# Token ids spread from 16 partitions, the folded table copied by ScalarE, and transposes that wait chunk by chunk

## The reference

```
h = relu(conv(emb_table[x]))                  # x: (2, 1024) ids under 125; 128 features; 2 taps, groups of 4
h = h + attention(layernorm(h))               # 8 heads of 64; its residual is the normed input
h = h + ffn(layernorm(h))                     # attention-like product, 8 experts, last product
```

## Time and profile before

| | us |
|---|---|
| median of 3 runs (386.87 to 386.99) | 386.97 |
| the profiled execution | 386.93 |
| its span | 385.1 |
| TensorE busy (share of the span) | 378.7 (98%) |
| VectorE | 274.7 (71%) |
| ScalarE | 276.6 (72%) |
| GpSimd | 294.0 (76%) |

### The profile page before, as it was taken

The page is one execution under the profiler, slowest core; times in us unless marked ns, Lnnn a source line. Parts: engine busy times, 40 slices in busy tenths (PEclk is TensorE's granted clock), DMA queues, the critical chain, the costliest instruction groups (busy, mean ns, idle before and its releaser), DMA issues.

```text
span 385.1 us, 6735 instructions
## 1 busy us (share of the span) xinstructions
PE 378.7 (98%) x2368; PEld 221.7 (58%) x2368; DVE 274.7 (71%) x485; ACT 276.6 (72%) x396; POOL 294.0 (76%) x145
## 2 busy tenths in 40 slices
PE   8999999999999999999999999999999999999996
PEld 7866544544555445445544644454455744599995
DVE  6997777787877787777777787877785446775223
ACT  3566656668868886987788688868886489337763
POOL 3080486949999999999999999999999699900021
PEclk9999999999999999999999999999999999999999
DMA  4001002101132041103010720172044105000001
GB/s 133 22 0 49 8 5 53 55 0 57 33 82 56 3 98 16 55 3 110 3 55 5 217 56 3 33 188 58 4 109 113 57 1 147 19 2 15 14 29 55
DMA packets 28245, 19.46 MB, mean 51 GB/s; under 512 B 21264, under 2 KB 23696, under 8 KB 28212
## 3 DMA queue, kind: packets, MB, share of 16 engines
q1 hardware_dynamic: 27636, 18.05, 18.4%
q10 hardware_dynamic: 576, 0.98, 0.8%
HBM read 17.72 MB, written 1.17 MB: 49 GB/s over the span
## 4 chain that ended last, share of the span: by engine, by line
PE 95%; DVE 3%; ACT 1%; issue 1%; DVEq 0%
PE psum L694 30%; PE psum L683 24%; PE psum L621 11%; PE psum L609 6%; PE psum L630 4%; PE psum L738 4%; PE psum L749 3%; PE psum L585 3%; PE psum L705 2%; PE psum L560 1%; PE psum L646 1%; PE psum L648 1%; PE psum L772 1%; PE psum L534 1%; DVE attn_out L1096 1%
## 5 line engine op out<-in xcount | busy, mean ns | idle before, releaser
L1132 DVE TENSOR_REDUCE half_maxes<-psum 128x1 f32<-128x512 f32 x232 | 149.0, 684 | 26.1 <-PE psum L621 24.5
L895 ACT ACTIVATE probs<-psum 128x1024 f32<-128x1024 f32 x128 | 124.8, 1022 | 54.9 <-PE psum L683 54.4
L694 PE MATMUL psum<-probs,v_all 128*64 128x512 f32 x512 | 123.7, 604 | 0.0
L1362 POOL TENSOR_TENSOR sums<-sums,probs 128x1024 f32<-128x1024 f32 x31 | 74.2, 2393 | 3.8 <-ACT probs L895 3.8
L1362 POOL TENSOR_TENSOR odd_sum<-odd_sum,probs 128x1024 f32<-128x1024 f32 x31 | 74.3, 2396 | 0.0
L694 PEld LDWEIGHTS psum<-probs,v_all 128*64 128x64 f32 x512 | 31.2, 136 | 62.3 <-issue 41.9
L1180 DVE TENSOR_SCALAR psum<-max_plane 128x512 f32<-128x512 f32 (+1 forms) x55 | 43.0, 791 | 30.9 <-ACT probs L895 30.9
L1362 POOL TENSOR_TENSOR sums<-probs 128x1024 f32<-128x1024 f32 x16 | 38.0, 2374 | 26.9 <-ACT probs L895 26.4
L621 PE MATMUL psum<-k_round,q_round 64*128 64x512 f32 x256 | 57.8, 450 | 0.6 <-DVE half_maxes L1132 0.5
L621 PEld LDWEIGHTS psum<-k_round,q_round 64*128 64x128 f32 x256 | 24.1, 183 | 53.8 <-DVE half_maxes L1132 42.9
L683 PE MATMUL psum<-q_round,k_round 64*128 64x512 f32 x256 | 52.4, 404 | 0.1
(11 more groups left out here) (131 smaller groups left out, 451.5 us busy)
## 6 DMA issues: line engine op xcount, KB each, us to landing
max_plane<-rows_scratch SPq DMA_DIRECT2D x16, 512.0 KB, 3.9
inv_sb<-inv_scratch SPq DMA_DIRECT2D x14, 256.0 KB, 5.3
max_rows_of<-maxes SPq DMA_DIRECT2D x128, 0.5 KB, 2.0
v_all<-in_fc SPq DMA_DIRECT2D x4, 512.0 KB, 7.5
fc_late<-in_fc SPq DMA_DIRECT2D x4, 512.0 KB, 7.4
out_h<-probs SPq DMA_DIRECT2D x7, 128.0 KB, 1.8
v_all<-in_w ACTq DMA_DIRECT2D x3, 256.0 KB, 3.7
woT<-in_wo SPq DMA_DIRECT2D x1, 256.0 KB, 3.5
```

The lines of the kernel that those rows point to most:

```text
L694: last = pe.matmul(out_bank[head_rows(h), :], v_all[:, s, kc, head_rows(h)], probs[unit(s, kc, half) % TILES][:, h, :], start=(kc == 0), s ...
L895: last = act.activation(probs[u % TILES][:, heads, :], source, ACT.Exp, scale=SCALE)
L1132: dve.reduce_max(half_maxes[:, h, qc, keys:keys + 1], slot[:, h, :], AX.X).then_inc(maxed, 1)
L1362: pool.tensor_tensor(chain[:, :, :], first[:, :, :], probs[kc][:, :, :], ALU.add).then_inc(own, 1)
```

## The change

- The ids are loaded as 16 rows of 128, one row to a partition, and converted as 16x128. The selector has 16 columns.
- Each group is spread by four products of 128 columns, each with its own selector column, in place of one of 512. The semaphore is raised by the last of the four.
- The warm-up has four products in place of six.
- The folding product stands behind the first group's spreading products, ahead of the second group's. Its result is copied by ScalarE, ahead of the rounding of the K weights, and no longer by VectorE between the one-hot comparisons.
- Each of the first eight transposes waits for its own chunk, in place of one wait for four.
- ScalarE's fourth rectifier stands behind the two roundings of the first sequence.

```diff
-WARM_START = 6
+WARM_START = 4
-        ids_rows = residual[0:NG, 0:GROUP, :].rearrange("p t c -> p (t c)")
-        ids_whole, row_select = xL[:, 0:BANK], xL[:, BANK:BANK + NG]
+        ids_rows = residual[0:NCH, 0, :]
+        ids_whole, row_select = xL[:, 0:CHUNK], xL[:, CHUNK:CHUNK + NCH]
-            sp.dma_start(ids_rows.bitcast(I32), x.rearrange("b (g n) -> (b g) n", g=NG // B)).then_inc(ids_loaded, 16)
+            sp.dma_start(ids_rows.bitcast(I32), x.rearrange("b (g n) -> (b g) n", g=KCH)).then_inc(ids_loaded, 16)
             def spread_ids(g):
-                pe.matmul(bank(IDS_BANK[g]), row_select[:, g:g + 1].broadcast_to([128, 128]), ids_whole,
-                          start=True, stop=True).then_inc(ids_spread, 1)
+                for j in range(GROUP):
+                    row = g * GROUP + j
+                    last = pe.matmul(bank(IDS_BANK[g])[:, j * CHUNK:(j + 1) * CHUNK], row_select[:, row:row + 1].broadcast_to([128, 128]),
+                                     ids_whole, start=True, stop=True)
+                last.then_inc(ids_spread, 1)
             spread_ids(0)
-            spread_ids(1)
             pe.wait_ge(consts_made, 1)
             pe.wait_ge(tables_loaded, 16)
             pe.matmul(bank(3)[:, 0:TAPS * C], embT, convT, start=True, stop=True).then_inc(folded_ready, 1)
+            spread_ids(1)
             spread_ids(2)
             spread_ids(3)
             for g in range(NG // B):
-                pe.wait_ge(x_normed, GROUP * (g + 1))
-                x_to_features(g, bank(FEATURE_BANK[g])).then_inc(xt_filled, 1)
+                for j in range(GROUP):
+                    pe.wait_ge(x_normed, GROUP * g + j + 1)
+                    last = pe.transpose(bank(FEATURE_BANK[g])[:, j * CHUNK:(j + 1) * CHUNK], x1[:, g * GROUP + j, :], ident[:, :])
+                last.then_inc(xt_filled, 1)
+            act.wait_ge(folded_ready, 1)
+            act.copy(folded[:, :], bank(3)[:, 0:TAPS * C]).then_inc(folded_sb, 1)
             act.wait_ge(w_loaded, 48)
             relu(2)
-            relu(3)
             for g in range(NG // B):
                 act.wait_ge(xt_filled, g + 1)
                 x_round(g, bank(FEATURE_BANK[g]))
+            relu(3)
-            dve.tensor_copy(row_select, ident[:, 0:NG])
+            dve.tensor_copy(row_select, ident[:, 0:NCH])
-            dve.tensor_scalar(ids_whole[0:NG, :], ids_rows.bitcast(I32), float(VOCAB - 1), 0.0, ALU.min, ALU.add).then_inc(ids_made, 1)
+            dve.tensor_scalar(ids_whole[0:NCH, :], ids_rows.bitcast(I32), float(VOCAB - 1), 0.0, ALU.min, ALU.add).then_inc(ids_made, 1)
             make_onehot(0)
             make_onehot(1)
-            dve.wait_ge(folded_ready, 1)
-            dve.tensor_copy(folded[:, :], bank(3)[:, 0:TAPS * C]).then_inc(folded_sb, 1)
             make_onehot(2)
             make_onehot(3)
```

## The result

| | before | changed |
|---|---|---|
| median, us | 387.06 (386.87 to 387.53, 6 runs) | 389.54 (389.36 to 390.51, 6 runs) |
| the profiled execution, us | 386.93 | 390.51 |
| its span, us | 385.1 | 388.7 |

The ratio is 1.0067, 95% interval [1.0054, 1.008]: slower by 2.5 us in the medians (2.6 by the ratio), where 386.7 was forecast in a range up to 388.8. The profiled execution is the slowest of the six, so its rows show 3.6 us, and about one of them is the luck of that execution.

What follows compares the result with a forecast made beforehand. TensorE was taken to bound the kernel, with 95% of the span; +0.04 us up to the convolution and -0.24 from transposes and rectifier gave -0.20, so 386.7 us, with a range for 8 in 10 of 386.0 to 388.8.

Steps and rivals of the forecast that it cites:

- part 3: Sixteen spreading products for four: load-bound, 0.112 us each (0.215 at 1.2 GHz), rise kept at 5.05; sum +0.04 us.
- rival B: TensorE's clock: rise only after twelve spreading products and eight convolution records, 2.0 us lost, 388.7 us; 12%.
- Part 1: Ids on 16 partitions: conversion stands behind GpSimd's memset and ends at 3.24 us.
- Part 2: Warm-up of four: streams until 2.77 us, hole of about 0.5 us, first spreading weight load at 3.30.
- Part 4: Folded table copied by ScalarE: 0.38 us, over by 5.6 to 5.8, hidden before the convolution, costing nothing.
- Parts 5 and 6: Chunk-wise transposes of the second group and fourth rectifier behind the roundings: K products earlier, sum -0.24 us.
- Rivals A and C: Spreading products: A, priced like plain f32, 388.5 us, 20%; C, at the pace of their columns, 386.0 us, 12%.

Runs made afterwards that it cites:

- a: Changed kernel with six warm-up products instead of four: 387.47 us median, ratio 1.0019.
- j: Changed kernel with GpSimd's two large memsets waiting for the converted ids, ten runs: ratio 1.0037, five at 386.5 to 386.8 us or so, others from 388.7.
- k: Changed kernel with five warm-up products instead of four: 389.5 us in four of four runs.
- o: Changed kernel with five warm-up products, the same kernel as k run again: median 387.15 us, seven early and three late.
- l: Changed kernel run again with no edit: 389.56 us, ratio 1.007.
- m: Kernel of b with twelve rounded-type products of 128 columns added between the fold and the second spreading product: 389.6 us, ratio 1.0067.
- b: Changed kernel with ids on 4 rows of 512 and four 512-column spreading products again, warm-up still four: 386.86 us, ratio 0.999.
- c: Kernel before with four warm-up products instead of six, nothing else: 387.27 us, ratio 1.0004.
- e: Changed kernel with 4 rows of 512 ids, four 512-column spreading products and six warm-ups: 386.47 us, ratio 0.9983.
- f: Kernel before with only the chunk-wise transposes and the fourth rectifier behind the roundings: 386.73 us, ratio 0.9992.
- i: Kernel of e with GpSimd's two large memsets behind the converted ids and five warm-ups: 386.45 us, ratio 0.9983.
- d: Changed kernel with its sixteen small spreading products in plain f32: 388.74 us, ratio 1.0048.
- n: Kernel of b with six plain f32 products of 128 columns added between the fold and the second spreading product: 388.44 us, ratio 1.0038.
- h: Changed kernel with GpSimd's two large memsets waiting for the converted ids, a single execution: 386.8 us.

## Why the prediction was wrong

**The step that failed** is one sentence of part 3: "I leave that moment where it is", the rise at 5.05 us. In the profiled execution it came at 12.8. All else in the sum up to it held. I had seen that the small products stream for half of the time and had put it into rival B at 12%, and what I held against it spoke of a hole only. The runs give the products the greater weight. They are in every kernel that has late runs, at 388.7 us and above (changed, a, j, k/o, l, m), while b, c, e, f and i have 51 runs, none above 388.2. (d and n carry dearer or added plain products, so their times start higher; in their traces the rise is at 5.1 and 7.0.) The hole alone (c) costs 0.2 us in the medians, and under 0.6 by its interval. How often the small products delay the rise goes with what TensorE did before them: late were 10 of 10 runs after four warm-ups and a hole of 0.5 us, 6 of 11 with the hole at 0.2, 7 of 14 after five warm-ups without a hole, 3 of 10 after six, 0 of 10 after eight. This order isn't shown to be more than a tendency. The sets of runs are from several chips: on the one that ran a and o, both have three late of ten, with six and with five warm-ups, while on the one that ran k, l and j all of k and l are late and six of ten of j. The number of warm-ups and the hole are told apart only in part: the changed kernel and j differ in the hole alone, against k and o it differs in both. Nor did I measure why a kernel's runs differ at all, so the cause of that stays open.

The Trainium skill's page "TensorE: Matmul & The Clock Gate", section "Part 1: The HAM clock gate (the "warmup" mystery)", says that the moment of the rise varies from run to run, by about half a microsecond to either side. The traces agree that it varies: in k and o, one kernel, it came at 11.1 and 9.9. They don't agree on how much. The two groups of times in a, up to 387.6 and from 389.3 us on, are 1.7 us apart, and a rise that moves by one microsecond moves the time by 0.5. The measurement decides.

**Price of B.** Put at 2.0 us, for twenty records at the slow pace. The profiled execution had about 11 spreading products and 24 convolution records at it, 35 x 0.101 = 3.5; the median run, 2.5 above before, had fewer. The range ended at 388.8 because I moved the rise only as far as the eighth record of the convolution; nothing in the rows said that it would come so soon.

**Part 1**: right. Conversion over at 3.23 to 3.25 for 3.24, and with 4x512 and the memset in its old place at 3.44 to 3.45 in every trace, whether the ids landed at 2.3 or at 2.8.

**Part 2**: right in its moments (start at 3.29), perhaps wrong in its worth. With the small products behind them, four warm-ups had 10 late runs of 10 and six had 3 of 10; with long products (b and e) the difference is 0.4 us in the medians, which the intervals don't separate.

**Part 3**: right in the pace, 0.112 us a product at 2.4 GHz (run a) and 0.213 at 1.2 GHz for 0.215; wrong in which of the two the twelve would get, since the clock rose too late.

**Part 4**: right, 0.37 us for 0.38, hidden. I had not seen what it is worth with long products: in run e the fold and its copy leave the path and the first convolution record ends 0.5 us earlier.

**Parts 5 and 6**: right, 0.22 in the medians of f and 0.27 in its trace, for 0.24.

**Rivals A and C**: refuted by run a's 0.112 us.

## What to carry to other kernels

Before TensorE has reached 2.4 GHz, what is put on it counts for more than its length: twelve records with twelve weight loads cost 1.2 us more in run m than in n, where the products in n stream for longer (by the estimate above, twice as long a record). So don't split a product into pieces that stream for less time than they occupy the engine in that stretch, and be wary of trimming the warm-up ahead of such pieces; and where a kernel's times fall into two groups, take many runs before believing one trace or one set of four (h, k). A forecast that holds the moment of the clock's rise fixed has to price the case that it moves by more than the part it moves past.

## What the runs showed of the hardware

- A product of the rounded type over 128 columns takes one record, and such records end 0.112 us apart at 2.4 GHz (run a) and 0.213 at 1.2 GHz (the changed kernel), as far apart as plain f32 records of 128 columns; that is half, and not a quarter, of the 512-column one's 0.427 at 1.2 GHz.
- The rise to 2.4 GHz came at 5.1 to 7.3 us in the eight traces without small products of the rounded type, and anywhere from 4.8 to 12.8 in the nine with them, while in the changed kernel TensorE was busy without a gap from 3.29 on.
- Each microsecond by which the rise is late costs 0.5 us (the four late traces).
- VectorE's int32 conversion of 4x512 takes 0.41 us alone and 1.11 when a GpSimd memset is under way (i and before); of 16x128, 0.21 (h) and 0.41 (the changed kernel).
